# The routed up product with the expert's weights standing and the gathered tokens moving, in a loop turned round

## The reference, cut to what matters

```python
x = x + ffn(cond(x))                             # x: 64 x 64 tokens of 512 numbers, 4096 tokens in all
# cond: x @ W.T plus a low rank product with the adapter of each sequence
# ffn, with xt = cond(x) as 4096 x 512:
sh_mid = gelu(einsum('th,ehd->ted', xt, Wsh_up));  shared = einsum('ted,edh->th', sh_mid, Wsh_down)   # 2 experts
probs  = softmax(xt @ W_router);  top_v, top_i = top_k(probs, 2)                                      # 16 experts
rt_mid = gelu(einsum('th,ehd->ted', xt, Wrt_up))                                                      # D = 256
routed = einsum('ted,edh->th', rt_mid * gate, Wrt_down)      # gate is not 0 for a token's two best experts only
out    = shared + routed
```

## Time and profile before

| what | value |
|---|---|
| runs | 790.14, 795.24, 790.97 us; median 790.97 us |
| span of the profiled execution | 791.7 us (no time of its own is given beside it) |
| TensorE matmul busy | 673.6 us, 85% of the span |
| TensorE weight load busy | 440.2 us, 56% |
| VectorE / ScalarE / GpSimd busy | 454.2 / 336.1 / 263.5 us (57 / 42 / 33%) |
| routed stage | from about 379 us (first transposes of gathered rows) to 668 us |
| mean granted TensorE clock | 0.919 over the span |

### The profile page before, as it was taken

The page is one execution under the profiler, slowest core; times in us unless marked ns, Lnnn a source line. Parts: engine busy times, 40 slices in busy tenths (PEclk is TensorE's granted clock), DMA queues, the critical chain, the costliest instruction groups (busy, mean ns, idle before and its releaser), DMA issues.

```text
span 791.7 us, 13966 instructions
## 1 busy us (share of the span) xinstructions
PE 673.6 (85%) x4115; PEld 440.2 (56%) x4117; DVE 454.2 (57%) x885; ACT 336.1 (42%) x480; POOL 263.5 (33%) x319
## 2 busy tenths in 40 slices
PE   5867677678888798778999999999999999989895
PEld 2434344335555465446566666666676667666462
DVE  2847755555445667996244444445444454378775
ACT  1233211144444557335645555555555555243320
POOL 1013311111111122742733333333333330777772
PEclk8978878877788889889999999999999999999998
DMA  6845555522322134330654554554545544999967
GB/s 242 312 174 193 185 194 187 188 80 84 117 91 80 53 119 148 106 133 13 201 173 144 147 152 141 157 147 144 154 140 156 148 145 143 373 319 330 362 223 252
DMA packets 49477, 135.61 MB, mean 171 GB/s; under 512 B 6000, under 2 KB 6000, under 8 KB 47024
## 3 DMA queue, kind: packets, MB, share of 16 engines
q1 hardware_dynamic: 38016, 97.86, 34.2%
q0 software_dynamic: 11440, 37.50, 17.0%
HBM read 86.31 MB, written 49.02 MB: 171 GB/s over the span
## 4 chain that ended last, share of the span: by engine, by line
PE 38%; issue 30%; POOL 16%; DVE 8%; DMA 4%; ACT 3%; POOLq 0%; SPq 0%; DVEq 0%; ACTq 0%
PE bank L1402 13%; PE bank L1421 12%; POOL rtw L617 8%; PE bank L1386 4%; PE bank L1411 3%; PE bank L1336 2%; PE bank L1264 2%; ACT act_in L686 2%; POOL arena L520 2%; POOL tmp L520 2%; DVE region L1121 1%; DMA region<-xc_dram,slot_idx 1%; DMA region<-w_r 1%; DVE region L1122 1%; POOL shw L525 1%
## 5 line engine op out<-in xcount | busy, mean ns | idle before, releaser
L1143 DVE SCALAR_TENSOR_TENSOR region<-bank,scale,region 128x512 f16<-128x512 f32 x79 | 59.2, 751 | 132.0 <-ACT region L821 132.0
L1402 PE MATMUL bank<-rtw,region 128*128 x948 | 117.2, 273 | 0.0
L1421 PE MATMUL bank<-rtw,tmp 128*128 x474 | 115.2, 379 | 0.3 <-DVE tmp L1151 0.3
L1336 PE MATMUL bank<-act_in,shw 128*128 128x256 f16 x768 | 91.7, 280 | 11.7 <-POOL act_in L549 8.3
L1402 PEld LDWEIGHTS bank<-rtw,region 128*128 128x128 f16 x948 | 89.3, 98 | 15.5 <-issue 1.5
L583 POOL DMA_INDIRECT region<-xc_dram,slot_idx x79 | 77.3, 979 | 61.3 <-POOL slot_idx L580 60.5
L1349 PE MATMUL bank<-shw,hid 128*128 128x512 f16 x384 | 87.2, 384 | 7.9 <-DVE rtw L1207 5.7
L1336 PEld LDWEIGHTS bank<-act_in,shw 128*128 128x128 f16 x768 | 76.3, 101 | 26.7 <-POOL act_in L549 8.9
L617 POOL DMA_INDIRECT rtw<-r_dram,row_idx x64 | 71.7, 1121 | 27.7 <-issue 16.6
L828 ACT ACTIVATE region<-bank,un_dn 128x512 f32<-128x512 f32 x79 | 54.3, 687 | 55.7 <-PE bank L1421 52.3
L817 ACT ACTIVATE tmp<-bank,un_up 128x256 f32<-128x256 f32 x79 | 37.5, 474 | 80.2 <-PE bank L1402 80.2
(11 more groups left out here) (159 smaller groups left out, 1004.5 us busy)
## 6 DMA issues: line engine op xcount, KB each, us to landing
r_dram<-region SPq DMA_DIRECT2D x79, 256.0 KB
rtw<-rt_w SPq DMA_DIRECT2D x16, 1024.0 KB, 7.4
act_in<-xT SPq DMA_DIRECT2D x16, 512.0 KB, 4.6
xc_dram<-rows SPq DMA_DIRECT2D x16, 512.0 KB, 5.9
xcT_dram<-hid SPq DMA_DIRECT2D x16, 512.0 KB, 2.9
rtw<-x_rows SPq DMA_DIRECT2D x16, 512.0 KB, 4.3
rtw<-xcT_dram SPq DMA_DIRECT2D x13, 512.0 KB
out<-rtw SPq DMA_DIRECT2D x9, 512.0 KB
```

The source lines that it names most:

```text
L1143: nc.vector.scalar_tensor_tensor(xgT[s][:, 1], R_XT[s][:].rearrange("p (k t) -> p k t", k=HK), col(scale, C_ALL).bitcast(F32), xgT[s][:, 0 ...
L1336: last = mm(UP[em % 2][:, 0:CHUNK], shw[:, e, w0:w0 + P], actT[s][:, xp, k, :], start=(k == 0 and n == 0), stop=(k == HK - 1 and n == 2))
L1402: last = mm(R_UP[s][:, 0:D], xgT[s][:, xp, k, :], rtw[:, bass.ds(e, 1), w0:w0 + D].rearrange("p a d -> p (a d)"), start=(k == 0 and n == 0 ...
L1421: last = mm(R_DN[s][:], midT[s][:, xp, m, :], rtw[:, bass.ds(e, 1), w0:w0 + H].rearrange("p a h -> p (a h)"), start=(m == 0 and n == 0), s ...
```

## The change

The up product changes places: the expert's weights stand (24 weight loads of 128 x 128) and the tokens move (24 matmuls of 128 columns). Its result has the 256 inner numbers on the partitions, in two blocks, and the tokens along the free dimension, which is how the down product wants its standing operand. So `r_transpose_mid` goes, and `split_midT` reads `mid[s]` in SBUF in place of the bank `R_MT[s]`. The gelu now has to wait until `split_midT` of tile j-2 has read `mid[s]`.

The loop on TensorE is turned round: a step is now down of j, up of j+2, transpose x of j+4. On VectorE `split_midT(j)` stands ahead of `low_xgT(j+2)`. `r_experts` loads four numbers for each pair.

```diff
-                dve.wait_ge(midT_psum, j + 1)
-                src = R_MT[s][:, 0:D].rearrange("p (m t) -> p m t", m=DM)
+                dve.wait_ge(r_gelu_ready, j + 1)
+                src = mid[s].rearrange("p (m t) -> p m t", m=DM)
...
-            def r_gelu(j, s):
+            def r_gelu(j, s, first=False):
+                if not first:
+                    act.wait_ge(midT_ready, j - 1)
...
             with dve.Fori(0, NJ_2 - 1) as i:
                 for s in range(2):
+                    split_midT(2 * i + s, s)
                     low_xgT(2 * i + s + 2, s)
-                    split_midT(2 * i + s, s)
...
-                for k in range(HK):
-                    for n, (xp, wp) in enumerate(PASSES):
-                        w0 = (UP_HI, UP_LO)[wp] + k * D
-                        last = mm(R_UP[s][:, 0:D], xgT[s][:, xp, k, :], rtw[:, bass.ds(e, 1), w0:w0 + D]...)
+                for m in range(DM):
+                    for k in range(HK):
+                        for n, (wp, xp) in enumerate(PASSES):
+                            w0 = (UP_HI, UP_LO)[wp] + k * D + m * P
+                            last = mm(R_UP[s][:, m * P:(m + 1) * P], rtw[:, bass.ds(e, 1), w0:w0 + P]...,
+                                      xgT[s][:, xp, k, :], ...)
...
-            def r_pair(i, first=False, more=True):
+            def r_round(i, first=False):
                 e = r_experts(i)
                 for s in range(2):
                     j = 2 * i + s
-                    r_transpose_mid(j, s, first and i == 0)
-                    r_up(j + 1, 1 - s, e[s + 1], first and i == 0 and s == 0)
-                    if more:
-                        r_transpose_x(j + 3, i + 1 + s, 1 - s)
-                    if first and i == 0 and s == 0:
-                        pe.wait_ge(shared_ready, NT * EARLY)
-                    r_down(j, s, e[s], first and i == 0)
+                    r_down(j, s, e[s], first)
+                    r_up(j + 2, s, e[2 + s])
+                    r_transpose_x(j + 4, i + 2, s)
...
+            for s in range(2):
+                r_up(s, s, e[s], first=True)
+                r_transpose_x(2 + s, 1, s)
+            pe.wait_ge(shared_ready, NT * EARLY)
             for i in range(2):
-                r_pair(i, first=True)
-            with pe.Fori(2, NJ_2 - 1) as i:
-                r_pair(i)
-            r_pair(NJ_2 - 1, more=False)
+                r_round(i, first=(i == 0))
+            with pe.Fori(2, NJ_2 - 2) as i:
+                r_round(i)
```

More of the change, by code:

```diff
@@ L244, in adaln_moe_kernel @@
         UP, DOWN = bank[1:3], bank[3:5]
-        R_XT, R_UP, R_MT, R_DN = [bank[0], bank[5]], bank[6:8], bank[2:0:-1], bank[3:5]
+        R_XT, R_UP, R_DN = [bank[0], bank[5]], bank[6:8], bank[3:5]
         w_adapters, w_mask, w_cond, w_shared = sem("w_adapters"), sem("w_mask"), sem("w_cond"), sem("w_shared")
@@ L278, in adaln_moe_kernel @@
         r_up_ready, r_gelu_ready = sem("r_up_ready"), sem("r_gelu_ready")
-        midT_psum, midT_ready = sem("midT_psum"), sem("midT_ready")
+        midT_ready = sem("midT_ready")
         r_dn_ready, rrow_ready = sem("r_dn_ready"), sem("rrow_ready")
@@ L830, in r_step @@
             def r_step(j, i, s, first=False):
-                r_gelu(j, s)
+                r_gelu(j, s, first and j < 2)
                 r_high(j + 2, s)
@@ L1157, in _ @@
                 for s in range(2):
+                    split_midT(2 * i + s, s)
                     low_xgT(2 * i + s + 2, s)
-                    split_midT(2 * i + s, s)
+            split_midT(NJ - 3, 0)
             low_xgT(NJ - 1, 0)
-            split_midT(NJ - 3, 0)
             low_condT(EARLY + 1, 1, early_condT(EARLY + 1))
@@ L1391, in r_experts @@
                 return nc.values_load_multi_w_load_instructions(
-                    tile_e[0:1, bass.ds(i, 1), 0:3].rearrange("p a m -> p (a m)"), engines=(mybir.EngineType.PE,), min_val=0, max_val=E_RT - 1,
+                    tile_e[0:1, bass.ds(i, 1), 0:4].rearrange("p a m -> p (a m)"), engines=(mybir.EngineType.PE,), min_val=0, max_val=E_RT - 1,
                     skip_runtime_bounds_check_because="a count of experts, cut off at the last one by the vector engine")[1]
@@ L1398, in r_up @@
                     pe.wait_ge(r_gelu_ready, j - 1)
-                for k in range(HK):
-                    for n, (xp, wp) in enumerate(PASSES):
-                        w0 = (UP_HI, UP_LO)[wp] + k * D
-                        last = mm(R_UP[s][:, 0:D], xgT[s][:, xp, k, :], rtw[:, bass.ds(e, 1), w0:w0 + D].rearrange("p a d -> p (a d)"),
-                                  start=(k == 0 and n == 0), stop=(k == HK - 1 and n == 2))
-                last.then_inc(r_up_ready, 1)
[L1406 to L1412, removed]
+                for m in range(DM):
+                    for k in range(HK):
+                        for n, (wp, xp) in enumerate(PASSES):
+                            w0 = (UP_HI, UP_LO)[wp] + k * D + m * P
+                            last = mm(R_UP[s][:, m * P:(m + 1) * P], rtw[:, bass.ds(e, 1), w0:w0 + P].rearrange("p a d -> p (a d)"),
+                                      xgT[s][:, xp, k, :], start=(k == 0 and n == 0), stop=(k == HK - 1 and n == 2))
+                last.then_inc(r_up_ready, 1)
             def r_down(j, s, e, first=False):
@@ L1443, in _ @@
             shared_down(2, 1)
-            r_up(0, 0, r_experts(0)[0], first=True)
-            r_transpose_x(2, 1, 0)
-            for i in range(2):
-                r_pair(i, first=True)
-            with pe.Fori(2, NJ_2 - 1) as i:
-                r_pair(i)
-            r_pair(NJ_2 - 1, more=False)
-            e = r_experts(NJ_2)
-            r_transpose_mid(NJ - 1, 0)
+            e = r_experts(0)
+            for s in range(2):
+                r_up(s, s, e[s], first=True)
+                r_transpose_x(2 + s, 1, s)
+            pe.wait_ge(shared_ready, NT * EARLY)
+            for i in range(2):
+                r_round(i, first=(i == 0))
+            with pe.Fori(2, NJ_2 - 2) as i:
+                r_round(i)
+            e = r_experts(NJ_2 - 2)
+            r_down(NJ - 5, 0, e[0])
+            r_up(NJ - 3, 0, e[2])
+            r_transpose_x(NJ - 1, NJ_2, 0)
+            r_down(NJ - 4, 1, e[1])
+            r_up(NJ - 2, 1, e[3])
+            e = r_experts(NJ_2 - 1)
+            r_down(NJ - 3, 0, e[0])
+            r_up(NJ - 1, 0, e[2])
+            r_down(NJ - 2, 1, e[1])
             shared_up(EARLY // 2, 0, blocks=range(1))
-            r_down(NJ - 1, 0, e[0])
+            r_down(NJ - 1, 0, e[2])
             shared_up(EARLY // 2, 0, blocks=range(1, EM))
```

## The result

The changed kernel takes **814.21 us** (median, 811.61 to 816.72) against 792.01 of the kernel before, run beside it: a ratio of 1.0259, 95% interval 1.0213 to 1.0305. It is slower, and 815 had been forecast, with a range of 801 to 833. The profiled execution took 816.18 us for a span of 814.4.

The account below looks back on a forecast made before the run. TensorE's sequencer becomes the bound: 6.1 us of work plus 2.0 for addresses, less savings, gives 7.7 a pair; 35 rounds and the tail add 23.6 to a span of 791.7, 815.3, so 815 us, range 801 to 830 (833 with the clock's case).

Parts of the forecast that it names:

- Which resource: Routed stage: TensorE's sequencer, 6.1 us of work per 7.0 us pair, is close behind the array and becomes the bound.
- The count and price of the addresses: Routed up product: 16 address computations a tile, 32 a pair, at 0.125 us: 4.0 us a pair against 2.0 before.
- The pair: Routed loop on TensorE: 7.7 us for each pair of tiles, ends 7.3 and 8.1, against 7.0 before.
- The array's part: Routed up product: 24 matmuls of 128 columns take 1.31 us, upper bound 2.64; the array needs 6.1 us a pair.
- The sum: From tile 6's transposes at 402.94, the last down product ends at 691 instead of 667.7; +23.6 gives a span of 815.3.
- The tail behind the loop: After 35 rounds: 11.3 us of sequencer work until up 78, then two down products and a shared block, ending at 691.
- The off-chain steps: Gelu, split, gathers and SyncE's stores stay hidden; VectorE's split halves take between half of 0.48 us and the same.
- Where the loss would be seen: Array waits in every up product and about 1 us at the loop's head; TensorE near 80% busy, clock 1.00.
- Cheap addresses: Rival: weight loads' addresses cost the sequencer no more than before; 6.4 us a pair, 768 us; chance 0.10.
- Weight loads that bind: Rival: up product's matmuls cost 0.11 us each with their weight loads; 8.8 us a pair, 858 us; chance 0.05.
- The clock: Rival: idle array lowers the routed stage's clock to 0.91; 50 us of it cost 18 more, 833 us; chance 0.07.
- the load's length: Loop's head: loading experts' numbers takes 0.9 to 0.96 us for three; the fourth is costed at nothing.

Follow-up runs that it names:

- experiment 1: Changed kernel, but the routed up product takes expert 0's weights from a fixed address for every tile; 764.36 us, ratio to before 0.9648.
- experiment 3: Kernel before, with the up product's moving weights taken in two halves: 24 matmuls of 128 columns, 16 addresses instead of 8; 827.74 us, ratio 1.0439.
- Experiment 4: Changed kernel with four rounds in one turn of TensorE's loop and one load of ten experts' numbers for them; 799.81 us, ratio 1.0099.
- experiment 9: Changed kernel's up product, without transposes of mid, in TensorE's old order (up j+1, transpose x j+3, down j), looped as before; 800.31 us, ratio 1.0083.
- experiment 5: Changed kernel with TensorE's rounds all written out instead of looped; 767.3 us, ratio to before 0.9684.

## Why the prediction was right, step by step

- **Which resource.** The forecast read the sequencer as second behind the array, at 6.1 us of work in 7.0. Shown by experiments 1 and 3: taking the up product's 32 computations a pair away brought 50 us and left the array as the bound, adding 16 to the kernel before cost 34 (40 had been expected; its load fell from 0.95 to 0.79 us at the same time, 6 us over 37 pairs).
- **The count and price of the addresses.** 16 a tile at 0.125 were forecast; 1264 in all at 0.12 were found. Right.
- **The pair.** 7.7 forecast, 7.66 found (35 turns between 407.6 and 675.9).
- **The array's part.** 1.31 us for 24 matmuls of 128 columns was taken over the bound of 2.64; it is 1.34, and 1.35 to 1.40 in the changed kernel. In experiment 1 that is 0.056 us for each pair of load and matmul. The 81 ns that the Trainium skill gives for it (TensorE: Matmul & The Clock Gate, "Back-to-back issue gap") don't hold here.
- **The sum.** 23.3 us were forecast from tile 6's transposes to the last down product (the prediction then adds 23.6, a slip of 0.3), 20.7 measured. The 35 pairs took 268.3 us and not 269.5, which gives 1.3 of the difference. The tail behind the loop took 14.0 and not 15.5, which gives the rest: its two loads take 0.34 us each, not 1.1 with what goes with them. Ahead of tile 6 and behind the last down product 2.1 us came on top that had been forecast as 0. That the time came within 1 us of the forecast is luck in part.
- **The off-chain steps.** Gelu, split, gathers and stores cost nothing, as forecast. The split's first half fell from 0.48 to 0.36 us with its source in SBUF.
- **Where the loss would be seen.** Wrong. The prediction has the array wait "in every up product", with TensorE busy near 80%, and names "up products of 1.3 us back to back" as a sign of being wrong. The up products took 1.35 and 1.40, and the matmuls were busy 43.05 of 50 us, 86%. By that sign alone one would have dropped a right theory: the 1264 computations and the pair of 7.7 decide, and the gap, 1.1 us a pair, stands in front of the round's first down product, under a wrong name. At about 1 us at the loop's head it had been forecast too. The down product, 1.30 us of the array for 0.6 of the sequencer, gives just the lead that the following up product, 1.34 for 2.0, uses up. The prediction names that lead, but not what it does to the place of the loss.
- **The rivals.** Cheap addresses: no, the full price was paid. Weight loads that bind: no. The clock: 1.00 in the changed kernel. Experiment 4, with stops of 3 us, shows that the case was a real one: 0.97 from 450 to 500 us, then 0.91 to 0.92.
- **What wasn't seen.** That the load's length was no constant. It was taken at its 0.9 with four numbers for three at no cost, and 0.84 was found. That was luck: where nothing else lengthened it, the load of four took 0.33. It hid two things: that three numbers cost 0.44 us more than four (16 us in the kernel before), and that turning the loop round cost 14 of the change's 22 us, as much as the longer load makes, while the forecast had put all of it on the addresses as if the order were free. With the old order the change comes out at 800 (experiment 9).

## What to carry to other kernels

Count what the sequencer does beside what the array does: operands at an address known only at run time cost 0.12 us of the sequencer for every different address, with 128, 256 and 512 columns alike, so halving the columns of such matmuls doubles that bill. Where a loop's head and the addresses set the pace, write the loop out or put several rounds in one turn before judging the change in it: the same change cost 22 us in its loop, and gained 9 when both kernels were written out. A wait put down to the instruction that ended last is to be checked against the order of the tiles. A busy share of matmuls near 100% doesn't show that they follow each other as fast as they can: divide the time of a group by its count.

## What the runs showed that was not expected

- A load of four numbers into TensorE's registers took 0.33 us at its best, of three never below 0.77, of ten 2.9 to 3.2. Reading one number too many made a kernel 1.8% faster.
- The same load of four took from 0.33 to 1.0 us, differently from kernel to kernel. Short loads went with quiet DMA queues and long ones with packets under way; the cause is open.
- A written out stage of 79 tiles ran without any visible stop for code: 50.00 of 50 us busy in its middle stretches, and no gap in its chain (experiment 5).
